# Graph attention: GpSimd makes complement masks for four node tiles of six heads

## The reference

```python
g = (h @ W_lin.T).reshape(n, 8, 32)
e = el[:, None, :] + er[None, :, :]        # el, er: g times the two halves of attn_w
e = where(e >= 0, e, 0.2 * e)
a = softmax(where(adj == 0, -inf, e), axis=1)
x = x + einsum('ijh,jhf->ihf', a, g)
```

## Time and profile before

| | us |
|---|---|
| median of 3 runs (2178.05 to 2183.5) | 2179.54 |
| the profiled execution | 2181.5 |
| its span, first to last instruction | 2179.8 |
| `gat_sums` in it, first matmul of line 924 to DVE's last line 888 | 170.7 to 665.8 |

### The profile page before, as it was taken

How to read it: one execution, slowest core, us unless ns; L and a number is a source line. 1 busy time by engine, 2 the same in 40 slices (tenths; PEclk the granted TensorE clock), 3 DMA queues, 4 the chain that set the end, 5 groups by cost and what they waited for, 6 DMA issues and landing times. The chain is left out here.

```text
span 2179.8 us, 58737 instructions
## 1 busy us (share of the span) xinstructions
PE 1967.2 (90%) x23674; PEld 1544.2 (71%) x23674; DVE 1870.4 (86%) x4135; ACT 1605.7 (74%) x1894; POOL 923.9 (42%) x966
## 2 busy tenths in 40 slices
PE   4848999999996899999896999999999999897999
PEld 3638999999995788888663666666666666566444
DVE  5667999999998899988677999999999999996222
ACT  4667999999995777542165999999999999895000
POOL 0020000000004444445315888888888888872000
PEclk9958999999997999999997999999999999998999
DMA  9987221221201156779554122211221122101222
GB/s 305 365 326 290 86 82 57 70 88 63 97 21 42 56 147 163 158 163 188 132 152 174 37 72 72 72 46 62 72 72 63 46 72 72 40 2 54 83 83 72
DMA packets 178078, 235.13 MB, mean 108 GB/s; under 512 B 112195, under 2 KB 143971, under 8 KB 174481
## 3 DMA queue, kind: packets, MB, share of 16 engines
q1 hardware_dynamic: 153408, 203.68, 30.5%
q10 hardware_dynamic: 24400, 27.70, 3.8%
HBM read 161.79 MB, written 49.00 MB: 97 GB/s over the span
## 5 line engine op out<-in xcount | busy, mean ns | idle before, releaser
L2207 DVE CUSTOM_DVE_ANT_0 h_S<-h_ps,off 128x832 f32<-128x832 f32 x832 | 800.4, 1018 | 17.3 <-PE h_ps L2106 15.4
L2106 PE MATMUL h_ps<-KS,QS 98*128 98x416 f16 x1664 | 442.4, 348 | 73.0 <-DVE h_mx L2207 42.3
L2166 ACT ACTIVATE h_H<-h_S,h_nmx 128x2048 fp8e4<-128x2048 f32 x208 | 416.7, 2003 | 70.3 <-DVE h_nmx L2213 70.3
L842 ACT ACTIVATE b_CA<-room,HC 128x1152 fp8e4<-128x1152 f32 (+1 forms) x384 | 435.5, 1219 | 0.0
L943 PE MATMUL b_pb<-xb,room 128*128 128x132 f16 x5408 | 416.0, 222 | 3.6 <-DVE room L904 3.2
L943 PEld LDWEIGHTS b_pb<-xb,room 128*128 128x128 fp8e4 x5408 | 341.8, 97 | 6.6 <-DVE room L904 6.1
L2060 POOL TENSOR_SCALAR h_gap<-h_S,h_nmx 128x1280 f32<-128x1280 f32 x208 | 277.2, 1332 | 91.6 <-DVE h_nmx L2213 81.9
L924 PE MATMUL b_pz<-xb,adjT 128*128 128x134 f16 x2704 | 258.5, 223 | 14.2 <-PEq L302 14.2
L2065 POOL TENSOR_SCALAR h_H<-h_gap 128x1280 uint8<-128x1280 f32 x208 | 260.5, 1253 | 17.2
L2137 PEld LDWEIGHTS h_po<-Vhl,h_HT 128*128 128x128 fp8e4 x5408 | 214.8, 98 | 65.0 <-ACT h_HT L2173 0.7
L2106 PEld LDWEIGHTS h_ps<-KS,QS 98*128 98x128 f16 x1664 | 96.1, 98 | 191.4 <-DVE h_mx L2207 117.3
(11 more groups left out here) (246 smaller groups left out, 3186.7 us busy)
## 6 DMA issues: line engine op xcount, KB each, us to landing
h_rows<-in_adj_dram SPq DMA_DIRECT2D x24, 1663.5 KB, 7.5
room<-in_adj_dram SPq DMA_DIRECT2D x25, 832.0 KB, 6.8
room<-in_adj_dram SPq DMA_DIRECT2D x25, 831.5 KB, 7.2
e_dram<-c_U ACTq DMA_DIRECT2D x78, 256.0 KB, 3.3
xb<-xv_dram SPq DMA_DIRECT2D x44, 435.5 KB, 5.0
adjT_dram<-adjT SPq DMA_DIRECT2D x1, 10816.0 KB, 32.4
c_ad<-adjT_dram SPq DMA_DIRECT2D x13, 832.0 KB, 6.9
m_ad<-adjT_dram SPq DMA_DIRECT2D x13, 832.0 KB, 4.5
```

The source lines that it names most:

```text
L842: nc.scalar.activation(dst[:, 0:cols], elr[:, n % 2, 0:cols], ACT.Sigmoid, bias=HC[:, h, 1, jt:jt + 1], scale=STEP, saturate=False).then_i ...
L2106: last = nc.tensor.matmul(ps[:, ch % 2, b, 0:SB], QS[:, i % 2, h, :], KS[:, h, c0:c0 + SB], start=True, stop=True)
L2166: nc.scalar.activation(H[:, g % 2, 0:CA], S[:, g % 2, 0:CA], ACT.Exp, bias=nmx[:, g % 2:g % 2 + 1], scale=1.0, saturate=False).then_inc(s_ ...
L2207: nc.vector.tensor_tensor_reduce(out=two(S[:, g % 2, ch * SW:(ch + 1) * SW]), in0=ps[:, ch % 2, :, 0:SB], in1=two(off[:, i % 2, ch * SW:(c ...
```

## The change

In a negated unit (jt 4, 10, 16 and 22, heads 2 to 7, in all three groups: 72 units) GpSimd subtracts the unit's slot of B from the adjacency, word by word, and so has the mask of the edges with e <= 0, in a ring CN of two slots. PE multiplies the slot of B by the 66 columns of f = 1, and CN by the 66 columns of f = 0, in 2 x 9 (or 2 x 8) matmuls instead of 9 (or 8). The f = 0 factors of these tiles and heads have their sign flipped, since the sum over e > 0 is subtracted later. The all-edge sums of pairs of heads 2 to 7 leave these four jt out. DVE's and ACT's work on masks and sums stays as it was.

```diff
@@ startup
-            pool.wait_ge(s_fac, 7)
+            pool.wait_ge(s_fac, 8)
...
                 nc.vector.tensor_scalar(vf[:], vf[:], VSC, None, ALU.mult).then_inc(s_fac, 1)
                 dve.wait_ge(s_fac, 7)
+                flipped = vf[:, 0, NEG.start:NEG.stop:NEG.step, 2:HEADS]
+                nc.vector.tensor_scalar(flipped, flipped, -1.0, None, ALU.mult).then_inc(s_fac, 1)
+                dve.wait_ge(s_fac, 8)
@@ constants
+NEG = range(4, NT - 2, 6)
+RING_CN = 2
@@ all_edges_schedule
-        gn = HEADS_IN[2 * m][1]
-        steps = [(b, jt) for b in range(-(-gn // 3)) for jt in range(NT)]
+        g0, gn, h = HEADS_IN[2 * m]
+        steps = [(b, jt) for b in range(-(-gn // 3)) for jt in range(NT) if not (h >= 2 and jt in NEG)]
@@ gat_sums
+    negated = [u for u, (n, jt) in enumerate(units) if HEADS_IN[n][2] >= 2 and jt in NEG]
...
+        CN = room[:, EW + BW:EW + BW + RING_CN * GN * P // 4].bitcast(FP8).rearrange("p (s n) -> p s n", s=RING_CN)
...
+        @block.gpsimd
+        def _(pool):
+            for i, u in enumerate(negated):
+                n, jt = units[u]
+                g0, gn, h = HEADS_IN[n]
+                pool.wait_ge(s_sel, u + 1)
+                if i >= RING_CN:
+                    pool.wait_ge(s_mm, negated[i - RING_CN] + 1)
+                nc.gpsimd.tensor_tensor(words(CN[:, i % RING_CN], gn), k.adjT[:, g0:g0 + gn, jt, :].bitcast(I32), words(B[:, u % RING_B], gn), ALU.subtract).then_inc(s_cn, 1)
...
                 pe.wait_ge(s_sel, u + 1)
+                if u in negated:
+                    i = negated.index(u)
+                    pe.wait_ge(s_cn, i + 1)
+                    for f, x in ((1, B[:, u % RING_B]), (0, CN[:, i % RING_CN])):
+                        for t in range(gn):
+                            b, at = t // 3, t % 3 * W + f * 2 * G1
+                            last = nc.tensor.matmul(pb[:, p, b, at:at + 2 * G1], x[:, t * P:(t + 1) * P], xb[:, m % 2, p, f, jt, 0:2 * G1],
+                                                    start=False, stop=False, skip_group_check=True)
+                    last.then_inc(s_mm, 1)
+                    continue
```

More of the change, by code:

```diff
@@ L734, in gat_sums @@
     tag = "b0"
-    s_mm, s_sel, s_ca, s_cd, s_y, s_t, s_all, s_z, s_adj = (
-        k.sem(f"s_{tag}_{n}") for n in ("mm", "sel", "ca", "cd", "y", "t", "all", "z", "adjT_out"))
+    s_mm, s_sel, s_ca, s_cd, s_cn, s_y, s_t, s_all, s_z, s_adj = (
+        k.sem(f"s_{tag}_{n}") for n in ("mm", "sel", "ca", "cd", "cn", "y", "t", "all", "z", "adjT_out"))
     s_x = [k.sem(f"s_{tag}_x{i}") for i in range(2)]
```

## The result

| | before | after |
|---|---|---|
| median of 4 runs, us | 2180.33 (2178.05 to 2183.50) | 2213.53 (2210.22 to 2215.88) |
| ratio to before | 1 | 1.0150 (95%: 1.0138 to 1.0162) |
| the profiled execution | 2181.5, span 2179.8 | 2213.3, span 2211.6 |

A forecast was written before the change was run, and what follows sets the result against it. PE was taken to bound heads of nine tiles, DVE 0.3 us behind, and DVE those of eight. DVE's losses of 24.6 and 12.7, plus 0.5 (end) and 0.2 (start), gave +38 us on 2179.5: 2217 us, range 2190 to 2250.

The forecast's parts named there:

- What bounds the kernel: Layer 0's sums: PE sets the pace with nine tiles, DVE 0.3 us behind; with eight DVE does, without slack.
- PE's side: Layer 0's sums: 18.4 us of matmuls saved, short matmuls at 30 ns; PE's head of nine tiles falls to 19.7 us.
- GpSimd's own time: Each of the 72 subtractions takes 0.78 us alone for 288 words, 0.73 for 256.
- rival of a slower integer path: GpSimd's subtraction takes 1.2 us and costs DVE 1.0: +68 us, about 2248 us; chance 15%.
- The price to DVE: Each subtraction takes 0.58 us (nine tiles) or 0.53 (eight) from DVE: 24.6 us in 12 heads, 12.7 in six.
- POOL gets its turn within one DVE operation: In the changed stretch GpSimd's subtraction waits only for the DVE operation under way, up to 0.73 us.
- Heads 0 and 1 don't change: Heads 0 and 1 of each of the three groups, six heads without negated units, keep their length.
- The added waits: PE waits for GpSimd's mask, up to 1.5 us late at the first such unit, then hidden; about 0.5 us remains.
- my last sign of being wrong: PE's waits for POOL as long at a head's fourth negated unit as at its first, and DVE waiting for PE.
- The end: End of the stage of sums: about 0.5 us is left of PE's added waits.
- PE pays each wait afresh: At each negated unit PE waits 0.4 us for DVE and 0.8 for POOL: +67 us, about 2247 us; chance 4%.
- The start: Layer 0's start: one more DVE operation of 24 elements behind line 651 costs 0.1 to 0.3 us, 0.2 in the sum.

The follow-up runs named there:

- e7: The kernel after run once more unchanged, for a second profile; 2211.96 us, ratio 1.0141 to before.
- e1: The kernel after, but GpSimd subtracts one word of each partition instead of 288, so the complement isn't made; 2197.14 us, ratio 1.0075 to before.
- e5: The kernel after, but GpSimd sets the complement slot to zero by memset instead of subtracting; 2173.86 us, ratio 0.9965 to before.
- e2: The kernel before with GpSimd's 72 subtractions added, whose result nobody reads; 2211.76 us, ratio 1.0143 to before.
- e6: The kernel after, but GpSimd copies the slot of B with one input instead of subtracting, complement left out; 2191.03 us, ratio 1.0042 to before.
- e8: The one-word version of the kernel after, plus a DVE wait for its own last result behind each negated unit; 2179.75 us, ratio 0.9997 to before.

## Why the prediction was right

The sign, the engine and the mechanism of the cost were right, though not every step beside it, and the sum of 38 us stands against 33 measured (31 in e7, without a lockout). DVE stayed full (100% at eight tiles from 540 to 640 us, 98% in the window with the lockout) and PE fell to 91%, as forecast. By steps:

- **What bounds the kernel.** DVE's slack in a head of nine tiles was put at 0.3 us (20.4 of 20.7). It was 0.43: 20.26 us in e1 and e5. In heads of eight tiles it was put at nothing, and 18.42 us before and in e5 are the same.
- **PE's side.** The short matmuls follow each other at 30 ns (the row below, the last one's own time 0.19 us: 0.42 / 14), as taken from layer 2. PE's work fell under DVE's as forecast, and the saving of 18 us was worth 7 at most (e5). The price of 81 ns for a pair of load and matmul, which the Trainium skill, TensorE: Matmul & The Clock Gate, "Back-to-back issue gap", gives, isn't seen.

```profile
319.82 0.61 PE L964 MATMUL b_pb<-xb,room 128*128 128x66 f16 x15
```

- **GpSimd's own time.** 0.78 us from float additions and multiplications; the shortest of 72 int32 subtractions, made while DVE stood, took 0.784. The rival of a slower integer path falls.
- **The price to DVE**, the term that carries the sum: 0.58 and 0.53 us were taken, 0.53 and 0.46 measured. The rule, own time less a hidden part, was right, and the hidden part was sized 0.20 us from layer 1's cast, where it is 0.26 here (e2, e6). 24.6 us were forecast for the 12 heads, 12 x 1.68 = 20.2 came (without the lockout); 12.7 for six, 10.6 came. Of the 4.4 us in the first, 12 x 4 x 0.05 = 2.4 are this size and 2.0 are DVE's slack, which was 0.43 us and not 0.3.
- **"POOL gets its turn within one DVE operation"** was wrong. It waited through two to four as a rule (up to 2.41 us recorded for 0.78) and once through 23. I had read it off a start-up in which DVE has gaps and a layer where it came after one. Of what it would show I had 1.4 us at most, and a line 904 or 857 lengthened: it was the comparison in 61 of 68, by 0.54 us. The lockout cost 4.9 us, which by luck fill most of what the price and the slack had too high.
- **"Heads 0 and 1 don't change"** was wrong by 2.3 us in six heads. Before, a unit's matmuls started 6.8 us behind its line 904 in the middle of heads 1 to 15, and PE set the pace. During the slower heads of after PE catches up (2.9 us behind in the middle of head 6), so in heads 8 and 9 DVE runs at its own 20.3 us and waits for nobody. Relieving PE isn't needed for that: in e2, where PE has all its work, they last 20.27 and 20.34 us too. Head 1 is another matter: 22.45 us before and in e2, 22.09 in after and e5, where PE has less to do.
- **The added waits.** PE's waits for the mask (4.2 us in 50) cost nothing: after's heads are as long as e2's, where PE has no such wait. But the reason given, a lag of PE that hides them once it is there, was wrong. PE is faster than DVE now and catches up within each head. It waits for GpSimd at neither the first nor the second negated unit of a head (but for the lockout and head 18), 0 to 1.4 us at the third and mostly 1.4 to 1.5 at the fourth. So the first half of my last sign of being wrong is met and more. The second half, that DVE waits for PE, is met in the lockout alone, which outlasts the 13 slots of the ring. The waits are harmless because PE has 22.4 - 19.7 = 2.7 us to spare in a head of nine tiles. Third and fourth negated unit of head 6, then the first of head 7:

```profile
325.00 0.70 PE L964 MATMUL b_pb<-xb,room 128*128 128x66 f16 x18 [0.49 <-POOL room L820]
331.41 0.70 PE L964 MATMUL b_pb<-xb,room 128*128 128x66 f16 x18 [1.46 <-POOL room L820]
337.80 0.71 PE L964 MATMUL b_pb<-xb,room 128*128 128x66 f16 x18
```

- **The end.** The end grew by 1.7 us where 0.5 were forecast, and most of that isn't PE's waits: in e2, where PE waits for no mask, it grew by 1.3 us.
- **A slip in a rival.** By its own 22.2 us for a head of eight, "PE pays each wait afresh" adds 22.2 - 18.4 = 3.8 us in six heads, not 3.6: 68 us in all. Nothing else hangs on it.
- **The start.** Line 651 to the first product went from 0.40 to 0.61 us, of which 0.18 us are the flip: 0.2 as forecast. Before, then after:

```profile
125.20 1.05 DVE L691 TENSOR_TENSOR xb<-s_GE,s_vf 128x858 f32<-128x858 f32 x1
...
124.24 0.37 DVE L651 TENSOR_SCALAR s_vf<-s_vf 128x416 f32<-128x416 f32 x1
...
124.64 0.18 DVE L654 TENSOR_SCALAR s_vf<-s_vf 128x24 f32<-128x24 f32 x1
124.85 1.05 DVE L694 TENSOR_TENSOR xb<-s_GE,s_vf 128x858 f32<-128x858 f32 x1
```

No version tried beats the kernel before except e5, which leaves the complement out. The cheapest right way to the complement found, DVE's own xor, costs DVE 0.37 us for each unit and is 0.8% slower than before.

## What to carry to other kernels

An idle GpSimd wasn't free capacity beside a DVE that never stops. Price an operation there by what it takes from DVE (here its own time less 0.26 us for a copy and a subtraction that read SBUF, nothing for a memset), and compare that with DVE doing it. And before a saving on the busiest engine is counted, look how close the next two are: here 18 us saved on PE could give 7. Where GpSimd must answer within a ring's depth of a gapless DVE, it can be shut out. One wait of DVE's for its own result (0.11 us) where GpSimd asks prevented that in e8, with an operation of one word; with the whole subtraction it wasn't tried.

## What the runs showed of the hardware that was not expected

- A GpSimd operation that has asked and waits isn't next in line: 22 DVE operations that started after it asked went ahead of one (11.22 us), 16 ahead of a one-word subtraction (8.04 us), until DVE had to stop. The Trainium skill, SBUF — State Buffer, "Who interferes with whom", says that whoever issues first gets the ports and the other waits until it ends; that the one waiting can be passed over again and again is not what it says, and the trace shows it.
- Without a lockout GpSimd got in nearly always just ahead of a comparison of DVE's (line 874), seldom between two line 921 (61 against seven).
- Two GpSimd operations back to back cost 0.53 + 0.60 us, not twice 0.53.
